# Five of eight key tiles of the value product as three fp32r products of high and low parts, in a gated cross-attention and feed-forward kernel

## The reference

```python
q_hk = (hidden_q @ Wq.T).reshape(b, s, H, K)
q_big = jnp.einsum('bshk,hkq->bshq', q_hk, w_kc_q)
kv_rope = kv_c * cos[None] + _rotate_half(kv_c) * sin[None]
q_r = jnp.einsum('bshq,hqr->bhsr', q_big, W_qr)
k_r = jnp.einsum('bld,hdr->bhlr', kv_rope, W_kr)
scores = jnp.einsum('bhsr,bhlr->bhsl', q_r, k_r)
attn = jax.nn.softmax(scores, axis=-1)
ctx_c = jnp.einsum('bhsl,bld->bhsd', attn, kv_rope)
ctx_lat = jnp.einsum('bhsd,hkd->bshk', ctx_c, w_kc_kv)
out = ctx_lat.reshape(b, s, H * K) @ Wo.T
```

## Time and profile before

| | us |
|---|---|
| median of 3 runs | 674.84 (673.44 to 675.44) |
| the profiled execution | 677.15, its span 675.4 |

### The profile page before, as it was taken

The page is one execution under the profiler, slowest core; times in us unless marked ns, Lnnn a source line. Parts: engine busy times, 40 slices in busy tenths (PEclk is TensorE's granted clock), DMA queues, the critical chain, the costliest instruction groups (busy, mean ns, idle before and its releaser), DMA issues.

```text
span 675.4 us, 9297 instructions
## 1 busy us (share of the span) xinstructions
PE 653.5 (97%) x2870; PEld 377.5 (56%) x2870; DVE 543.9 (81%) x882; ACT 356.8 (53%) x571; POOL 259.7 (38%) x232
## 2 busy tenths in 40 slices
PE   9798999999999999999999999999999898999997
PEld 8564555665665555565655555555555454445553
DVE  5787877788868885888698979997999886998873
ACT  3564664455445544554545454545454533498875
POOL 4822265133223222322235443332333352686651
PEclk9999999999999999999999999999999998999999
DMA  8108885788498849884988688869688763000001
GB/s 299 63 1 218 234 226 117 226 237 228 108 241 243 220 105 243 231 215 109 239 245 207 184 225 237 212 168 238 163 214 230 172 149 101 1 0 32 17 33 48
DMA packets 45206, 112.77 MB, mean 167 GB/s; under 512 B 11888, under 2 KB 15088, under 8 KB 45040
## 3 DMA queue, kind: packets, MB, share of 16 engines
q1 hardware_dynamic: 43712, 110.01, 61.5%
q10 hardware_dynamic: 1392, 2.29, 1.0%
q0 software_dynamic: 64, 0.00, 0.0%
HBM read 45.16 MB, written 2.10 MB: 70 GB/s over the span
## 4 chain that ended last, share of the span: by engine, by line
PE 48%; DVE 30%; ACT 7%; SPq 6%; POOL 3%; issue 3%; DMA 2%; PEld 1%; POOLq 0%; DVEq 0%; ACTq 0%; PEldq 0%
DVE E L1765 9%; PE ps_b L1392 9%; PE ps_s L1371 7%; DVE small L1755 7%; PE ps_ctx L1392 7%; ACT E L1580 6%; SPq L1096 5%; PE ps_s L586 5%; DVE wq L1781 2%; PE ps_b L1265 2%; POOL E L1160 2%; DVE x_sb L1745 2%; PE ps_b L1267 2%; PE ps_b L637 2%; PE ps_b L1266 2%
## 5 line engine op out<-in xcount | busy, mean ns | idle before, releaser
L1160 POOL TENSOR_SCALAR E<-E,small 128x1024 f32<-128x1024 f32 x128 | 151.1, 1190 | 346.7 <-DVE small L1760 346.6
L1580 ACT ACTIVATE E<-ps_s,small 128x1024 f32<-128x1024 f32 x128 | 142.3, 1113 | 209.0 <-DVE small L1755 177.5
L1765 DVE STREAM_TRANSPOSE E<-E 128x1024 f32<-128x1024 f32 x124 | 152.8, 1233 | 27.9 <-POOL E L1160 27.8
L1755 DVE TENSOR_REDUCE small<-ps_s 128x1 f32<-128x1024 f32 x128 | 149.1, 1203 | 4.5 <-PE ps_s L1371 4.4
L1392 PE MATMUL ps_ctx<-G,kv 128*128 128x512 f32 x256 | 123.2, 599 | 0.0
L1392 PE MATMUL ps_b<-G,kv 128*128 128x512 f32 x256 | 119.9, 598 | 2.1 <-DMA G<-E 2.1
L1392 PEld LDWEIGHTS ps_b<-G,kv 128*128 128x128 f32 x256 | 48.0, 190 | 51.8 <-issue 46.0
L1392 PEld LDWEIGHTS ps_ctx<-G,kv 128*128 128x128 f32 x256 | 46.4, 189 | 43.0 <-issue 40.3
L1265 PE MATMUL ps_b<-b_hi,ctx_hi 128*128 128x512 f32 x128 | 66.4, 519 | 0.6 <-DVE ctx_lo L1717 0.6
L1371 PE MATMUL ps_s<-k_hi,q_hi 64*128 64x512 f32 x256 | 57.3, 443 | 4.6 <-ACT E L1580 3.6
L586 PE MATMUL ps_s<-wq,q12T 128*128 128x512 fp8e4 x256 | 61.1, 385 | 0.1
(11 more groups left out here) (199 smaller groups left out, 960.9 us busy)
## 6 DMA issues: line engine op xcount, KB each, us to landing
G<-E SPq DMA_DIRECT2D x496, 128.0 KB, 2.4
w_stage<-in_wffn SPq DMA_DIRECT2D x48, 512.0 KB, 4.4
wo_s<-in_woT SPq DMA_DIRECT2D x8, 512.0 KB, 5.3
wq_s<-in_wq SPq DMA_DIRECT2D x7, 512.0 KB, 6.3
wkcq_s<-in_wkcqT SPq DMA_DIRECT2D x7, 384.0 KB, 4.5
out<-x_sb SPq DMA_DIRECT2D x8, 256.0 KB, 2.0
x_sb<-in_x SPq DMA_DIRECT2D x3, 512.0 KB, 5.9
wqr_s<-in_wqr SPq DMA_DIRECT2D x7, 192.0 KB, 5.4
```

What stands on the lines that cost most here:

```text
L1160: nc.gpsimd.tensor_scalar(e, e, rowinv[:, k:k + 1], 1.0, ALU.mult, ALU.mult).then_inc(scaled, 1)
L1580: nc.scalar.activation(out, scores, ACT.Exp, bias=negmax[:, k:k + 1], accum_out=rowsum[:, k:k + 1]).then_inc(exp_done, 1)
L1755: nc.vector.tensor_reduce(negmax[:, k:k + 1], ps_s[:, t % 2, :], AX_X, ALU.max, negate=True).then_inc(max_done, 1)
L1765: nc.vector.transpose(e_tile(w % 2, t), e_tile(w % 2, t)).then_inc(blocks_turned, 1)
```

## The change

- Of the eight key tiles of a unit, tiles 0 to 4 are multiplied as three fp32r products, tiles 5 to 7 stay native. TensorE takes them in the order 5, 0, 6, 1, 2, 3, 7, 4 (`STEP_TILE`).
- For each such tile ScalarE copies the tile of G to a high part (`split_high`, 128 x 512), in a ring `g_hi` of two buffers, and GpSimd subtracts it (`split_low`, 128 x 512 into `G_lo`). TensorE waits for the low part ahead of all three products. `HIGH_STEPS` puts the copies of tiles 0 to 4 at ScalarE's steps 0, 0, 2, 4, 5; at step 2 the copy stands behind the exponential of tile 2 of unit w+2. The copy of tile 2 waits for TensorE to be through with tile 0 (the ring), that of 3 with 1, that of 4 with 2.
- GpSimd's order in a unit: scale tile 1, low 0, low 1, low 2, scale tiles 2 and 3, low 3, low 4, scale tile 0.
- `cut_kv` splits the context once, on GpSimd, ahead of the first unit.
- The keys' product is one native product with `wkr_s` and a single `kvT`. This drops ScalarE's and VectorE's splitting of `wk` in each pair and VectorE's `kvT_lo` in the prologue. SyncE loads `wkr_s` for pair p+2 in slot 2, after the last keys' product of the pair, not in slot 1.
- The splitting of the normalised x (`xn_low`, `join_xn`) is cut in halves that stand in other slots of GpSimd.

```diff
+SPLIT, RING = 5, 2
+STEP_TILE = (5, 0, 6, 1, 2, 3, 7, 4)
+HIGH_STEPS = (0, 0, 2, 4, 5)
...
-WK_AT = (0, 1)
...
-        kvT_hi = sa("kvT_hi", [P, BATCH, LCTX], F32R)
-        kvT_lo = sa("kvT_lo", [P, BATCH, LCTX], F32R)
+        kvT = sa("kvT", [P, BATCH, LCTX])
...
-        wk_hi = sa("wk_hi", [P, 2, R], F32R)
-        wk_lo = sa("wk_lo", [P, 2, R], F32R)
         wkr_s = sa("wkr_s", [P, 2, R])
+        with ExitStack() as place:
+            kv_hi = place.enter_context(nc.sbuf_tensor("kv_hi", [P, BATCH, LT, DC], F32R))
         kv = sa("kv", [P, BATCH, LT, DC])
+        kv_lo = sa("kv_lo", [P, BATCH, SPLIT, DC], F32R)
+        g_hi = sa("g_hi", [P, RING, NF], F32R)
+        with ExitStack() as place:
+            G_lo = place.enter_context(nc.sbuf_tensor("G_lo", [P, 2, 4, ST, KEYS_Q], F32R))
...
+        def high_part(w, i):
+            return g_hi[:, (w + i) % RING, :]
...
-                    sp.wait_ge(wk_ready, p + 2)
+                if w == 2 and not (variant == "last" or isinstance(p, int) and p == 6):
+                    sp.wait_ge(side_done, side_index(p, variant, ("k", 1, 1)) + 1)
                     load_kr(sp, p + 2)
...
-            sp.wait_ge(wk_ready, 1)
+            sp.wait_ge(side_done, 8)
...
+        def cut_kv(pool, b):
+            whole, part = kv[:, b, 0:SPLIT, :], g_hi[:, :, :].rearrange("p a f -> p (a f)")[:, 0:SPLIT * DC].rearrange("p (l d) -> p l d", d=DC)
+            pool.wait_ge(kvt_psum, 2 * b + 2)
+            if b:
+                pool.wait_ge(kv_cut, 3)
+            nc.gpsimd.tensor_copy(part, whole).then_inc(kv_cut, 1)
+            pool.wait_ge(kv_cut, 3 * b + 1)
+            nc.gpsimd.tensor_tensor(kv_lo[:, b, :, :], whole, part.bitcast(F32), ALU.subtract).then_inc(kv_cut, 1)
+            pool.wait_ge(kv_cut, 3 * b + 2)
+            nc.gpsimd.tensor_copy(kv_hi[:, b, 0:SPLIT, :], part.bitcast(F32)).then_inc(kv_cut, 1)
+        def split_low(pool, p, w, i):
+            tile = g_tile(w % 2, i)
+            pool.wait_ge(split_hi, SPLIT * 4 * p + (SPLIT * w + i + 1))
+            pool.sem_inc(pool_passed, 1)
+            nc.gpsimd.tensor_tensor(g_tile(w % 2, i, G_lo), tile, high_part(w, i).bitcast(F32).rearrange("p (t i q) -> p t i q", t=ST, i=4),
+                                    ALU.subtract).then_inc(split_lo, 1)
         def pool_pair(pool, p, last=False):
             for w in range(4):
                 second, first = not (last and w >= 2), not (last and w >= 1)
-                for at, t in enumerate((1, 2, 3, 0)):
-                    if second if t else first:
-                        pool_scale(pool, *unit_ahead(p, w, 2 if t else 3), t)
-                    if at == 0:
-                        if is0(p) and w in XN_LOW_SLOTS:
-                            xn_low(pool, XN_LOW_SLOTS.index(w))
-                        for b in range(BATCH):
-                            if isinstance(p, int) and (p, w) == XN_JOIN_SLOTS[b]:
-                                join_xn(pool, b)
-                    if last and (w, at) == (1, 2):
-                        ln2_root(pool, 0)
-                if last and w == 1:
-                    atanh_end(pool)
+                u2, u3 = unit_ahead(p, w, 2), unit_ahead(p, w, 3)
+                if is0(p) and w == 0:
+                    split_low(pool, p, w, 0)
+                if second:
+                    pool_scale(pool, *u2, 1)
+                if not (is0(p) and w == 0):
+                    split_low(pool, p, w, 0)
+                split_low(pool, p, w, 1)
+                if last and w >= 2:
+                    ln2_root(pool, w - 2)
+                if last and w == 3:
+                    rms_root(pool, 1)
+                split_low(pool, p, w, 2)
+                if second:
+                    pool_scale(pool, *u2, 2)
+                    pool_scale(pool, *u2, 3)
                 if last and w == 2:
                     rms_root(pool, 0)
                     pool.wait_ge(ld_g, 32)
                     normed(pool, -2, 0)
+                split_low(pool, p, w, 3)
+                if last and w == 2:
                     normed(pool, -1, 1)
-                    ln2_root(pool, 1)
-                    rms_root(pool, 1)
+                split_low(pool, p, w, 4)
+                for i in range(2 * BATCH):
+                    if is0(p) and w == XN_LOW_SLOTS[i]:
+                        xn_low(pool, i)
+                    if isinstance(p, int) and (p, w) == XN_JOIN_SLOTS[i]:
+                        join_xn(pool, i)
+                if first:
+                    pool_scale(pool, *u3, 0)
+                if last and w == 1:
+                    atanh_end(pool)
...
-            for t in range(ST):
-                pool_scale(pool, 0, 1, t)
+            cut_kv(pool, 0)
+            pool_scale(pool, 0, 1, 0)
+            pool_scale(pool, 0, 1, 1)
+            cut_kv(pool, 1)
+            pool_scale(pool, 0, 1, 2)
+            pool_scale(pool, 0, 1, 3)
             pool_scale(pool, 0, 2, 0)
...
-                pe.wait_ge(wk_ready, 1 if at is not None else p + 2)
+                pe.wait_ge(ld_kr, 16 if at is not None else 16 * p + 32)
                 if at is not None:
                     pe.wait_ge(kvt_ready, 2 * b + j + 1)
                 cols = slice(j * NF, (j + 1) * NF)
-                wh = wk_hi[:, :, :].rearrange("p a r -> p (a r)")
-                wl = wk_lo[:, :, :].rearrange("p a r -> p (a r)")
-                nc.tensor.matmul(into, wh, kvT_hi[:, b, cols], start=True, stop=False)
-                nc.tensor.matmul(into, wl, kvT_hi[:, b, cols], start=False, stop=False)
-                last = nc.tensor.matmul(into, wh, kvT_lo[:, b, cols], start=False, stop=True)
+                last = nc.tensor.matmul(into, wkr_s[:, :, :].rearrange("p a r -> p (a r)"), kvT[:, b, cols], start=True, stop=True)
...
                 if is0(p) and w == 0:
+                    pe.wait_ge(kv_cut, 6)
                     first_tiles_copied(pe)
                 pe.wait_ge(exchanged[w % 2], 2 * EXCHANGE * p + EXCHANGE * (w // 2 + 1))
                 if not (is0(p) and w < 2):
                     pe.wait_ge(ctx_done, 4 * p + (w - 1))
-            turned = G[:, w % 2, :, :, key_tile(c)].rearrange("p i t q -> p t i q")
-            last = nc.tensor.matmul(CTX_PS[w % 2].rearrange("p (t i q) -> p t i q", t=ST, i=4), kv[:, w // 2, c, :], turned,
-                                    start=(c == 0), stop=(c == LT - 1))
+            b, tile = w // 2, STEP_TILE[c]
+            turned, into = g_tile(w % 2, tile), CTX_PS[w % 2].rearrange("p (t i q) -> p t i q", t=ST, i=4)
+            if tile < SPLIT:
+                high = high_part(w, tile).rearrange("p (t i q) -> p t i q", t=ST, i=4)
+                pe.wait_ge(split_lo, SPLIT * 4 * p + (SPLIT * w + tile + 1))
+                nc.tensor.matmul(into, kv_hi[:, b, tile, :], high, start=(c == 0), stop=False)
+                nc.tensor.matmul(into, kv_lo[:, b, tile, :], high, start=False, stop=False)
+                last = nc.tensor.matmul(into, kv_hi[:, b, tile, :], g_tile(w % 2, tile, G_lo), start=False, stop=(c == LT - 1))
+                if tile < SPLIT - 1:
+                    last.then_inc(split_done, 1)
+            else:
+                last = nc.tensor.matmul(into, kv[:, b, tile, :], turned, start=(c == 0), stop=(c == LT - 1))
             if c == LT - 1:
                 last.then_inc(pv_done, 1)
...
+        def split_high(act, p, w, i):
+            if i == 0:
+                if is0(p) and w == 0:
+                    act.wait_ge(kv_cut, 6)
+                else:
+                    act.wait_ge(split_done, 4 * (SPLIT - 1) * p + (SPLIT - 1) * w)
+                act.wait_ge(exchanged[w % 2], 2 * EXCHANGE * p + EXCHANGE * (w // 2 + 1))
+            elif i == 1:
+                if not (is0(p) and w == 0):
+                    act.wait_ge(pv_done, 4 * p + w)
+            else:
+                act.wait_ge(split_done, 4 * (SPLIT - 1) * p + ((SPLIT - 1) * w + i - 1))
+            copy_act(high_part(w, i).rearrange("p (t i q) -> p t i q", t=ST, i=4), g_tile(w % 2, i)).then_inc(split_hi, 1)
...
+                    if c == 0:
+                        split_high(act, p, w, 0)
                     if c == 0 and w:
...
-                    if (w, c) == WK_AT and variant != "last":
-                        wk_high(act, 16 * p + 32)
+                    for i in range(1, SPLIT):
+                        if c == HIGH_STEPS[i]:
+                            split_high(act, p, w, i)
...
+            def kvt_copy(g):
                 b, half = divmod(g, 2)
                 act.wait_ge(kvt_psum, g + 1)
-                copy_act(key_columns(kvT_hi[:, b, half * NF:(half + 1) * NF]), by_tile(KVT_BANK[g])).then_inc(kvthi_ready, 1)
+                copy_act(key_columns(kvT[:, b, half * NF:(half + 1) * NF]), by_tile(KVT_BANK[g])).then_inc(kvt_ready, 1)
...
-        def wk_low(dve, ready):
-            dve.wait_ge(wkhi_ready, ready)
-            lo_part(wk_lo[:, :, :], wkr_s[:, :, :], wk_hi[:, :, :]).then_inc(wk_ready, 1)
...
```

(5 more changed lines are left out.)

53 lines of the change are left out of this document (21 added, 32 removed).

## The result

| | before | after |
|---|---|---|
| median of 4 runs | 674.14 us (673.44 to 675.44) | 746.16 us (742.61 to 750.26) |
| the profiled execution | 677.15 | 742.61, its span 740.8 |

The forecast was 719 us, and the time lies 1 us above the top of the range, 745. A run more than 1.5% above the fastest of its kernel (one of four in experiment 6) is left out of medians and ratios.

A forecast was written before the change was run, and what follows sets the result against it. TensorE, 97% busy, was taken as the bound. 677.15 (profiled) + 34 (pairs 0 to 6) - 1 (pair 7) - 0.5 (prologue) + 2 (rounding) + 10 (clock) = 721.7, so 719 us as a median; range 690 to 745.

The forecast's parts named there:

- the step that gave pair 7 -1 us: Last pair: products save up to 3.3 us, partly taken back by ring delay and GpSimd's feed-forward steps; -1 us, -3 to +3.
- That TensorE was the bound, and that any wait would come on top: Whole kernel: TensorE, busy 97% of the span, has no wait left to lose; a slot lasts its products plus added waits.
- The products: Value and keys' products: three fp32r cost 0.69 us, one native 0.86; split tiles -3.3, keys +0.7, net -2.6 us a pair.
- The wait ahead of tile 2: TensorE waits for tile 2's low part 1.9, 3.2, 2.3 us in slots 1 to 3, none in slot 0: 7.4 a pair.
- Tiles 3 and 4, and tiles 0 and 1, come early enough: Every slot: TensorE has 4.7 us between tiles 2 and 3; tiles 0 and 1 are needed 3.4 us or more after the slot's start.
- a sign of being wrong: Forecast wrong if gaps ahead of tile 2 are under 1 us each, or TensorE waits for tiles 3, 4 or the exchange.
- Pairs 0 to 6 have the pattern: Pairs 0 to 6: each loses 4.8 us net (7.4 of waits against 2.6 saved), +34 us in all.
- The clock, seven losses at 1.5 us: TensorE's clock drops once a pair behind the 3.2 us wait: 7 x 1.5 = +10 us; ends none and +36.
- The rounding, +2 us: Pairs 4 to 6: VectorE's weight rounding slows subtractions by up to 0.4 us in nine slots, at most 3.6; +2 taken.
- the larger price: Pairs 4 to 6: a subtraction could wait for a whole rounding, 1.09 us, adding some 6 us over nine slots; not counted.
- The range's top: Whole kernel: upper end of 745 us, from three losses of clock a pair.
- one rival alone, the clock's: Same waits, but TensorE's clock falls behind each, three losses a pair: 719 + 26 = 745 us, chance 0.16.

The follow-up runs named there:

- experiment 6: The changed kernel with pair 7 multiplied natively as before, its tiles neither copied nor subtracted: 728.62 us, ratio 1.078 to the kernel before.
- experiment 2: The changed kernel with a ring of three buffers instead of two and tile 2's copy at ScalarE's step 0: 690.91 us, ratio 1.025 to the kernel before.
- Experiment 3: The kernel before with only the keys' part of the change (one native keys' product), value product all native: 677.07 us, ratio 1.0032.
- Experiments 1: The changed kernel with tile 2's copy at ScalarE's step 1, ahead of the exponential, instead of step 2: 705.41 us, ratio 1.047 to the kernel before.
- experiment 4: The changed kernel with two zero-weight products ahead of tile 2's wait in slots 1 to 3 of pairs 0 to 6: 734.90 us, ratio 1.089.
- 5: The changed kernel with TensorE waiting for the low part only ahead of a tile's third product: 733.13 us, ratio 1.091 to the kernel before.
- Experiment 7: The changed kernel with units 2 and 3 of pair 0 multiplied natively, neither copied nor subtracted: 741.74 us, ratio 1.099 to the kernel before.
- Experiment 8: The changed kernel with a ring of three buffers and also pair 0's first unit multiplied natively: 690.46 us, against 690.91 with the ring of three alone.

## Why the prediction was wrong, point by point

The waits of the middle pairs were right. What failed is the step that gave pair 7 -1 us, with ends of -3 and +3: it cost some +14. Pair 0, put down as a pair like the others, cost 5.6 us more than the forecast for one.

- **That TensorE was the bound, and that any wait would come on top**: right. TensorE's idle time grew from 21.9 to 84.8 us, 62.9 of the 65.4 us of new span.
- **The products** (0.69 for three, 0.86 native): right by the distances of starts. The saving in clean pairs was 1.3 us in experiment 2, 2.6 by my count. Experiment 3 has the keys' part as forecast; of the missing 1.3 us, 0.95 in pair 2 and 0.6 in pair 1 are short waits that I had at nothing, and what takes the rest isn't shown.
- **The wait ahead of tile 2** (1.9, 3.2, 2.3 and 0 us in slots 1, 2, 3, 0): measured in pairs 1 to 6 as 1.6 to 2.2, 2.7 to 3.4, 2.1 and 0. Experiments 1 and 2 show the cause, 4 its price without the clock, 5 that GpSimd's subtraction ends it. Right.
- **Tiles 3 and 4, and tiles 0 and 1, come early enough**: right in the middle, wrong at the ends, which I had not worked through: pair 0 waits 3.2 us for tile 0 and 1.6 us for tile 3, pair 7 for both as well. The prediction had named waits for tile 3 as a sign of being wrong.
- **Pair 7, -1 us with ends of -3 and +3**: the step that failed. Experiment 6 prices it at +14 in the stretches of the trace, the tail with it (17.5 between medians). I had counted the missing exponentials of slots 2 and 3 as relief and not asked what covers the waits: in slot 0 it was the next pair's side tasks, and between tiles 2 and 3 the scores of a later unit, and the last pair has neither. GpSimd's feed-forward steps had no price of their own beside the new ones; what they cost isn't separated by any run.
- **"Pairs 0 to 6 have the pattern"**: wrong for pair 0, by 5.6 us. Two things differ there: an opening where value products come before scores, and a GpSimd with four operations of 2.4 us on xnT to do. Experiment 7 shows that most of the excess is in the later half: 7.1 us came back, two losses of clock among them, where two common slots would give 3. Experiment 8, with a ring of three, that freeing the opening gives nothing, as other waits stand behind it. How the excess divides in the changed kernel itself wasn't tried further.
- **The clock, seven losses at 1.5 us**: there were ten more than before, at 1.2 to 1.4 us each (experiment 4), so +12 to +14 where I had +10. Five of them are in pairs 1 to 5, as many as forecast, but that is luck: I had put one in each pair, behind slot 2's wait. Pair 1 has none and pair 5 two, and only two of the five stand at slot 2's wait; the others are at waits of 2.0 and 2.1 us in slots 1 and 3. The rest are at the ends, where the waits I missed stand, and are part of the 5.6 and 14.6 us. The Trainium skill (TensorE: Matmul & The Clock Gate, "HAM oscillation — how this bites in real kernels") describes a loop whose recurring waits, of some 3 to 5 us, throttle the clock every time. The waits here are mostly shorter, 1.5 to 3.7 us, and pair 1 has waits of 2.0, 2.7 and 2.1 us and no loss, so at this size it isn't each time.
- **The rounding, +2 us**: pairs 4 and 5 are within 0.5 us of the forecast, but the extra isn't where I had put it. The wait ahead of tile 2 in slot 2 is 3.4 us in pairs 4 to 6 and 2.7 in pairs 1 to 3, while the subtraction that ends it takes 1.30 and 1.26 us. What comes later is the exponential: S+4.23 in pair 4, S+3.63 in pair 2. In pair 4 two foldings of ScalarE (2.19 us from 385.00) stand ahead of the keys' high part, and VectorE's maxima stand behind the keys' low part. The 160 subtractions take 1.25 to 1.57 us, median 1.29. Their durations, minimum, median and maximum:

```profile
L1217 POOL TENSOR_TENSOR G_lo<-G,g_hi x160: 1251/1286/1571, 52.0 to 635.6; 128x512 fp32r<-128x512 f32 x160
```

  The longest one, between two roundings, in order of time:

```profile
373.23 0.67 DVE L1851 TENSOR_SCALAR wq<-w_stage 128x1024 fp8e4<-128x1024 f32 x1
373.44 1.57 POOL L1217 TENSOR_TENSOR G_lo<-G,g_hi 128x512 fp32r<-128x512 f32 x1 [3.62 <-DVE small L1830]
374.55 1.02 DVE L1851 TENSOR_SCALAR wq<-w_stage 128x1024 fp8e4<-128x1024 f32 x1
```

  Ten subtractions start while a rounding runs, 0.18 to 0.46 us before its end, and they are the longer the more of it is left (1.30 us with 0.18 left, 1.57 with 0.46). The ten roundings that start inside a subtraction take 0.74 to 1.02 us instead of 0.69. None of the ten subtractions has a whole rounding ahead of it, so the larger price that I worked out in the prediction never fell due. The rule that GpSimd and a VectorE operation in a two-port mode fully block one another (the Trainium skill, SBUF — State Buffer, "Who interferes with whom") agrees with these rows.

- **The range's top**: it was one rival alone, the clock's. It had no room for the ends and the clock at once, and the ±3 for pair 7 was not worked out from rows as the waits of the middle were.

## What to carry to other kernels

When a step is added between producer and consumer, find the consumer's wait in the order of the queues and not in busy shares: both engines that got the work had some 40% idle time, and of the 72 us that the change cost, 41 came back when one copy of 0.63 us moved ahead of one exponential. Work the first and the last turn of a loop through as separate cases: what covers a wait in the middle (work for the next turn) is missing in the last, and 20 of 65 us were lost at the two ends beyond the forecast. And before a wait is called the price of something, ask what stands right behind it; taking away 5 us of waits in the opening gave 0.5 us.
